# The row term of a graph-attention score, moved from TensorE transposes to a DMA through memory and a ScalarE copy

## What is computed

```python
mask = adjacency_matrix.astype(jnp.float32) + jnp.eye(n, dtype=jnp.float32) > 0
for l in range(attn_w.shape[0]):
    si = x @ attn_w[l, :d]
    sj = x @ attn_w[l, d:]
    scores = si[:, :, None] + sj[:, None, :] + attn_b[l]
    scores = jnp.where(scores >= 0, scores, 0.2 * scores)
    scores = jnp.where(mask, scores, -jnp.inf)
    attn = jax.nn.softmax(scores, axis=-1)
    agg = jnp.einsum('bij,bjd->bid', attn, x)
    h = layernorm(x + agg, g1[l], beta1[l])
    ff = jax.nn.gelu(h @ W1[l] + b1[l], approximate=False) @ W2[l] + b2[l]
    x = layernorm(h + ff, g2[l], beta2[l])
```

## Time and profile before

| | |
|---|---|
| median of 3 runs | 2259.94 us (2259.12 to 2261.8) |
| the profiled execution | 2259.16 us, span of its trace 2257.0 us |
| busy in the span | PE 97%, DVE 83%, ACT 84%, POOL 85% |
| chain that ended last | PE 83% of the span, DVE 12% |
| mean granted TensorE clock | 0.997 of full speed |
| DMA | 144.71 MB, 64 GB/s over the span |

### The profile page before, as it was taken

How to read it: one execution, slowest core, us unless ns; L and a number is a source line. 1 busy time by engine, 2 the same in 40 slices (tenths; PEclk the granted TensorE clock), 3 DMA queues, 4 the chain that set the end, 5 groups by cost and what they waited for, 6 DMA issues and landing times.

```text
span 2257.0 us, 46173 instructions
## 1 busy us (share of the span) xinstructions
PE 2199.1 (97%) x15464; PEld 1520.3 (67%) x15464; DVE 1868.8 (83%) x5886; ACT 1887.4 (84%) x3496; POOL 1914.8 (85%) x1644
## 2 busy tenths in 40 slices
PE   3999999999999999999999999999999999999998
PEld 2666766666666666666666666666666666666665
DVE  6889887788998787878999877777899978787874
ACT  5888888889888888888889888888898988888874
POOL 5788888889998888888999888888999888888896
PEclk9999999999999999999999999999999999999999
DMA  5432221135562112213654221122456221211253
GB/s 145 119 82 52 52 36 38 35 61 97 105 121 52 38 34 39 34 38 71 111 108 98 48 37 36 37 36 41 87 109 125 46 41 34 39 34 38 52 94 66
DMA packets 382266, 144.71 MB, mean 64 GB/s; under 512 B 312144, under 2 KB 380368, under 8 KB 382032
## 3 DMA queue, kind: packets, MB, share of 16 engines
q1 hardware_dynamic: 366192, 126.04, 27.3%
q0 software_dynamic: 15840, 15.73, 4.8%
HBM read 49.96 MB, written 16.78 MB: 30 GB/s over the span
## 4 chain that ended last, share of the span: by engine, by line
PE 83%; DVE 12%; issue 2%; DVEq 0%
PE p_hid L459 38%; PE p_pair L473 37%; PE p_pair L511 5%; DVE g_lo L712 2%; DVE bn L719 2%; PE p_pair L497 2%; DVE res L795 2%; DVE adj_in L740 2%; DVE dots L757 1%; DVE dots L760 1%; DVE p_lo L807 1%; PE p_pair L484 0%; DVE mv L724 0%; DVE var_eps L726 0%; DVE s_j L760 0%
## 5 line engine op out<-in xcount | busy, mean ns | idle before, releaser
L473 PE MATMUL p_pair<-w_hi,g_hi 128*128 128x256 f16 x3072 | 837.4, 273 | 0.0
L473 PE MATMUL p_pair<-w_hi,g_lo 128*128 128x256 f16 x3072 | 837.4, 273 | 0.0
L473 PE MATMUL p_pair<-w_lo,g_hi 128*128 128x256 f16 x3072 | 837.4, 273 | 0.0
L577 ACT ACTIVATE p_hid<-p_hid,b_eff 128x512 f32<-128x512 f32 x768 | 503.4, 655 | 282.7 <-PE p_hid L459 281.1
L712 DVE TENSOR_TENSOR g_lo<-p_hid,g_hi 128x512 f16<-128x512 f32 x768 | 517.4, 683 | 43.5 <-ACT g_hi L582 35.6
L459 PE MATMUL p_hid<-hT_hi,w_hi 128*128 128x512 f16 x1536 | 458.6, 380 | 22.1 <-DVE g_lo L712 17.4
L582 ACT ACTIVATE g_hi<-p_hid 128x512 f16<-128x512 f32 x768 | 458.7, 597 | 24.3
L459 PE MATMUL p_hid<-hT_lo,w_hi 128*128 128x512 f16 x1536 | 457.8, 380 | 0.5 <-DMA hT_lo<-h_lo 0.3
L459 PE MATMUL p_hid<-hT_hi,w_lo 128*128 128x512 f16 x1536 | 458.1, 380 | 0.0
L981 POOL TENSOR_TENSOR rstd<-var_eps,minus_half 128x4 f32<-128x4 f32 x224 | 228.5, 1020 | 244.3 <-DVE minus_mean L727 244.1
L473 PEld LDWEIGHTS p_pair<-w_hi,g_hi 128*128 128x128 f16 x3072 | 300.6, 98 | 106.5 <-issue 0.3
(11 more groups left out here) (77 smaller groups left out, 3574.0 us busy)
## 6 DMA issues: line engine op xcount, KB each, us to landing
out<-w_f SPq DMA_DIRECT2D x31, 512.0 KB, 4.1
x_in<-in_x SPq DMA_DIRECT2D x30, 512.0 KB, 6.9
w_f<-in_x POOLq DMA_DIRECT2D x30, 512.0 KB, 7.6
adj_in<-in_adj SPq DMA_DIRECT2D x32, 256.0 KB, 3.3
w_f<-in_L_gnn_W SPq DMA_DIRECT2D x6, 1024.0 KB, 7.0
hT_hi<-h_hi SPq DMA_TRANSPOSE x96, 3.1
hT_lo<-h_lo SPq DMA_TRANSPOSE x96, 3.1
pT_hi<-p_hi SPq DMA_TRANSPOSE x94, 2.4
```

The costliest lines, as they stand in the source:

```text
L473: mm = pe.matmul(ff_banks(s)[:, t, :], g[i][:, nodes], w[l][:, c, :], start=(c == 0 and t % 2 == 0 and n == 0), stop=(c == C - 1 and n == ...
L577: act.activation(p_hid[k][:], p_hid[k][:], ACT.Gelu, bias=b1_eff[:, l, c:c + 1], scale=1.0 / WSCALE).then_inc(gelu_ready, 1)
```

## The change

The row term of items 4 and on is no longer made by PE. SP writes `s_j` (128 partitions by 4 numbers) to a small buffer in memory, graph by graph, then reads those 512 numbers back as one row of 2 KB onto every partition (`sj_rows`), and ACT copies that tile into the PSUM bank where the transposes wrote before. `add_scores` reads the bank as before.

ACT's copy comes at c = 2 of slot s for item s+3, ahead of `norm_attention`. PE's wait for `res2` of item s-1 goes from PE's stream, and the same wait stands ahead of the copy in ACT's stream. To give the way through memory its time, the dot products run a slot earlier (item s+5 in slot s), and with them `norm_input` (s+5), `input_statistics` (s+6) and the loads of x. `make_mask` stays at s+4. The bias fold writes to another bank half, all of it in one slot, and PE's wait for it moves to `aggregate`.

In the opening `first_input(3)`, half of the low weights and the sum of two residual rows leave their places: the sum is now an adding DMA from POOL, `low_weights(0, 3)` and `first_input` of items 4, 5 and 6 lie in slot 0, whose DVE stream also has the dot products of items 4 and 5.

```diff
+        sj_rows = sb("sj_rows", [P, T, N])
+        sj_memory = [nc.dram_tensor(f"sj_memory{i}", [T, N], F32).ap() for i in range(2)]
...
+            def sj_to_memory(r, s):
+                sp.wait_ge(dots_ready, total(r, s, 8, 8))
+                if later(r, s, 6):
+                    sp.wait_ge(sj_in, sj_total(r, s - 2))
+                with nc.allow_non_contiguous_dma("four bytes of each node and graph"):
+                    sp.dma_start(sj_memory[s % 2].rearrange("t n -> n t"), s_j[s % RING][:]).then_inc(sj_out, 16)
+
+            def sj_to_rows(r, s):
+                sp.wait_ge(sj_out, sj_total(r, s))
+                if later(r, s, 5):
+                    sp.wait_ge(sj_rows_ready, total(r, s - 1, 1, 1))
+                sp.dma_start(sj_rows[:].rearrange("p t n -> p (t n)"),
+                             sj_memory[s % 2].rearrange("t n -> (t n)").partition_broadcast(P)).then_inc(sj_in, 16)
+
             def slot(r, s):
+                first = isinstance(r, int) and (r, s) == (0, 0)
+                if is_item(r, s + 4) and not first:
+                    sj_to_memory(r, s + 4)
                 if is_item(r, s + 2):
                     turn_probs_hi(r, s + 2)
...
-                if is_item(r, s + 4) and layer_of(s + 4) == 0 and group_of(r, s + 4) + 2 < G:
-                    sp.wait_ge(x0_ready, group_total(r, s + 4, 4, 4))
-                    load_x(group_of(r, s + 4) + 2)
+                if is_item(r, s + 5) and layer_of(s + 5) == 0 and group_of(r, s + 5) + 2 < G:
+                    sp.wait_ge(x0_ready, group_total(r, s + 5, 4, 4))
+                    load_x(group_of(r, s + 5) + 2)
                 if is_item(r, s + 1):
                     turn_h_lo(r, s + 1)
...
+                if is_item(r, s + 4):
+                    sj_to_rows(r, s + 4)
...
             def spread_sj(r, s):
 
                 pe.wait_ge(dots_ready, total(r, s, 8, 8))
-                if later(r, s, 4):
-                    pe.wait_ge(res2_ready, total(r, s - 4, 2, 2))
...
-                    if c == 4 and is_item(r, s + 3):
-                        spread_sj(r, s + 3)
+                    if isinstance(r, int) and (r, s, c) == (0, 0, 4):
+                        spread_sj(0, 3)
...
+            def rows_to_bank(r, s):
+                act.wait_ge(sj_in, sj_total(r, s))
+                act.wait_ge(res2_ready, total(r, s - 4, 2, 2))
+                act.activation(sj_bank(r, s), sj_rows[:], ACT.Copy).then_inc(sj_rows_ready, 1)
+
...
+                    if c == 2 and is_item(r, s + 3) and later(r, s):
+                        rows_to_bank(r, s + 3)
                     if c == 2 and is_item(r, s + 1):
                         norm_attention(r, s + 1)
...
-                    if c == 3 and is_item(r, s + 4) and layer_of(s + 4) == 0:
-                        norm_input(r, s + 4)
+                    if isinstance(r, int) and (r, s, c) == (0, 0, 3):
+                        norm_input(0, 4)
+                    if c == (4 if isinstance(r, int) and (r, s) == (0, 0) else 3) and is_item(r, s + 5) and layer_of(s + 5) == 0:
+                        norm_input(r, s + 5)
...
-                starts = is_item(r, s + 5) and layer_of(s + 5) == 0
+                starts = is_item(r, s + 6) and layer_of(s + 6) == 0 and not (isinstance(r, int) and (r, s) == (0, 0))
...
-                    if c == 6 and is_item(r, s + 4):
-
-                        dot_products(r, s + 4, 0)
-                        dot_products(r, s + 4, 1)
+                    if isinstance(r, int) and (r, s, c) == (0, 0, 4):
+                        low_weights(0, 3)
+                        dot_products(0, 4, 0)
+                        dot_products(0, 4, 1)
+                    if c == 6 and is_item(r, s + 5):
+
+                        dot_products(r, s + 5, 0)
+                        dot_products(r, s + 5, 1)
...
                 first_input(2)
-                first_input(3)
                 first_residual(0)
                 dot_products(0, 1, 0)
                 dot_products(0, 1, 1)
                 low_weights(0, 0)
+                low_weights(0, 1)
                 first_scores(1)
-                low_weights(0, 1)
+                first_input(3)
```

More of the change, by code:

```diff
@@ L379, in slot @@
                     weights(2, (s - 5) // 2)
+                if first:
+                    sj_to_memory(r, s + 4)
+                if is_item(r, s + 4):
+                    sj_to_rows(r, s + 4)
             def attention_rows(layers):
@@ L506, in aggregate @@
                     pe.wait_ge(score_steps, total(r, s + 1, 5, 4))
+                if isinstance(r, int) and r == 0 and s + 1 in FOLD_AT:
+                    pe.wait_ge(bias_ready, FOLD_AT[s + 1] + 1)
                 if later(r, s, 3):
@@ L860, in slot @@
                         hidden(r, s, c)
-                    if isinstance(r, int) and (r, s, c) == (0, 0, 0):
-                        first_input(4)
                     if c == 0 and is_item(r, s + 2):
@@ L874, in slot @@
                         dot_products(0, 3, 1)
+                    if isinstance(r, int) and (r, s, c) == (0, 0, 2):
+                        first_input(4)
+                    if isinstance(r, int) and (r, s, c) == (0, 0, 3):
+                        first_input(5)
                     if isinstance(r, int) and (r, s, c) == (LOOPS, PER - 1, 3):
@@ L895, in slot @@
                         aggregates(1, total(r, s + 2, 10, 8))
[L896 to L899 removed]
+                    if isinstance(r, int) and (r, s, c) == (0, 0, 4):
[5 more added lines that the diff above has]
+                        dot_products(r, s + 5, 1)
+                    if isinstance(r, int) and (r, s, c) == (0, 0, 7):
+                        first_input(6)
                     if isinstance(r, int) and (r, s, c) == (0, 2, 7):
@@ L1061, in slot @@
                     low_X(r, s + 2)
+                if first:
+                    first_deviation(5, 0)
                 if is_item(r, s + 1):
@@ L1066, in slot, with residual_rows @@
                     first_mask(s + 4)
+            def residual_rows(layers):
+                pool.dma_start(res_rows[:, layers].rearrange("p l d -> p (l d)"),
+                               b2[layers].rearrange("l d -> (l d)").partition_broadcast(P),
+                               accum_op=ALU.add).then_inc(res_rows_ready, 16)
             def first_deviation(i, n):
```

80 lines of the change are left out of this document (39 added, 41 removed).

## The result

The changed kernel takes **2293.8 us** (2292.6 to 2295.8) against 2260.0 for the kernel before on the same chip: ratio 1.0151, with a 95% interval of 1.0139 to 1.0163. It is 34 us slower. The forecast was 2279 in a range of 2236 to 2298. The profiled executions have spans of 2290.7 and 2257.0.

A forecast was written before the change was run, and what follows sets the result against it. PE's stream, busy 97% of the span, was taken as the bound, with DVE the bound in turn slots. Transposes -26, opening -6 and turns +52 gave +20 on 2259.16, so 2279 us, range 2236 to 2298.

The forecast's parts named there:

- 55 plain slots: Slots 8 to 18, 29 to 42, 53 to 66, 77 to 92: each loses PE's 0.44 us of transposes, 24.2 in all.
- slots 28, 52, 76: Slots with the mask but, after the change, neither statistics nor norm: from 22.80 to 22.15 us, 2.0 gained in all.
- three turns: Slots 19 to 27, 43 to 51, 67 to 75, layer 2 to 0: ACT's wait delays DVE, +17.3 us each, +52 together.
- opening to the end of slot 7: First slots: two waits bound the gain at 11 us, DVE's added work costs 7.1; taken as -6, ends -12 and +3.
- three waits in a full slot: Turn slots with mask, statistics and norm: DVE waits 1.9, 1.2 and 0.55 us for high halves of chunks 3, 4, 5.
- the mask's 0.21: In slots 28, 52 and 76: the delay by the mask, counted as gone after the change along with the transposes.
- R: Mid-slot time when DVE ends res2 of item s-1, for which ACT's copy waits; 1121.13 in slot 46.
- 6 us of room: The rows' two DMAs per item: 22 - 10 - 6 leaves 6 us before ACT wants them, so they cost nothing.
- The wait doesn't bind: Rival for the turn slots: ACT's lateness meets no one, so turns lose the transposes too; 2213 us, chance 10%.
- DVE's instructions get shorter: Rival for the turns: POOL's idle time shortens mask and low_probs, full slots 24.4 to 24.8; 2239 us, chance 14%.
- PE goes slower: Rival for some 20 turn slots: pauses drop PE to the 1.2 GHz level, up to 1.3 us each; 2305, chance 8%.
- The rows come late: Rival for every slot: the first DMA takes much longer than 5.4 us and ACT stands; 2330 or more, chance 3%.

The follow-up runs named there:

- e3: The kernel before with only ACT's wait for the residual of item s-1 added ahead of the attention norm, no copy or DMA: 2310.4 us, ratio 1.0225.
- e1: The changed kernel with ACT's copy and its wait moved from chunk 2 to behind chunk 3: 2228.2 us, ratio 0.9862 to the kernel before.
- e2: The changed kernel with the attention norm put ahead of ACT's wait and copy at chunk 2: 2243.4 us, ratio 0.9928 to the kernel before.
- e5: The changed kernel with the transposes back on PE, without DMAs, copy and its wait; reordered opening and slot-ahead order kept: 2254.3 us, ratio 0.9973.
- e6: The kernel with the copy behind chunk 3, with item 4's row term on PE and without its write and rows: 2221.6 us, ratio 0.9831.
- e4: The kernel with the copy behind chunk 3, with item 4's rows issued behind the probabilities' transposes in slot 1: 2230.2 us, ratio 0.9865.
- e8: The kernel with the copy behind chunk 3, with the DMA that brings the rows back issued twice per item: 2228.4 us, ratio 0.9866.

## Why the prediction was right in its sign, and 15 us short

Term by term, from the slots' own lengths in the two profiled executions:

| term of the sum | predicted | measured |
|---|---|---|
| 55 plain slots | -24.2 | -21.3 |
| slots 28, 52, 76 | -2.0 | +1.0 |
| three turns | +52 | +52.0 |
| opening to the end of slot 7 | -6 | +2.0 |
| sum | +20 | +33.7 |

**The turns: right, in mechanism and size.** The three waits in a full slot were put at 1.9, 1.2 and 0.55; they are 2.06, 1.02 and 0.49. A full slot was put at 26.35 and takes 26.39, one with the mask and the norm at 24.5 and takes 24.40, the nine at 225.7 and take 225.7. e3 shows that the wait alone does it, e1 that without its place nothing else does, e2 that the first wait goes by itself and leaves the other two. That the 225.7 is met to the tenth is luck: from residual to residual the same nine take 227.8 and not 227.05 (slot 19 takes 23.9 instead of 23.5, slot 27 23.2 instead of 22.8), and what is more there falls into slot 28. The step that carried this was to go through ACT's queue behind the wait and compare each high half with the time at which DVE wants it.

**Plain slots: right for 52 of 55.** They take 22.15. Slots 9 to 11 take 22.79, 23.18 and 23.16. The step that failed is the count: the slots behind the opening were called plain without looking at what else stands in them (weights are split up to slot 11, and DVE is busy 19.93 in slot 10 instead of 17.55); in e1 the same three take 22.15, so it is the wait that they pay for.

**Slots 28, 52 and 76: wrong by 1.0 each.** The prediction let them lose the transposes and the mask's 0.21 as well. They kept the mask's part (22.38 in e1) and had 0.8 of the wait on top (23.16). The mask alone makes DVE late enough for R to matter; the prediction had said so for slot 27 and not for the next.

**The opening: mis-sized by 8.** Up to the start of slot 8, the reordering brings -2.5 (e5; the prediction had -4), the seven transposes -3.1 (7 x 0.44). Against these stand two costs. Slot 1 of the changed kernel takes 29.11 and not e5's 25.54 less 0.44, which is +4.0:

```profile
71.37:100.48 29.11, 23.00 (x157) 14.80 (x158) 24.47 (x86) 22.50 (x47) 17.55 (x13) 1.00 0.64 147
```

PE stands there 2.64 us for the low probabilities' transpose and 1.02 for a `g_lo`. Slots 2 to 7 take 145.15, and 141.45 in e1, where ACT's wait stands a chunk later: +3.7. In e3 the wait alone costs these six slots 4.0. Together that is +2.1, and +1.96 was measured. So two steps failed. The DMA was costed at nothing in a plain slot, by 6 us of room, and the opening was never gone through with it: there the first write needs some 12 us and not 5.4, with five loads of rows for the other layers issued just ahead of it, and what is queued behind SP's wait is wanted at once. And the wait for R was to take some of 3 us in slots 1 to 3; it took 3.7, 3.3 of it in slots 5 to 7, where weights are split as in slots 9 to 11.

The prediction's own range for the sum, 2264 to 2297, isn't what the ends of its terms add up to, 2260 to 2296.

**The rivals.** *The wait doesn't bind*: no, but 2213 for a kernel without it was near: e6 takes 2221.6. *DVE's instructions get shorter*: the mask in slot 46 still takes 1.38 us, in a slot 3 us longer, as in the earlier trace rows. POOL stood idle elsewhere in the slot, but beside the mask (1130.02 to 1131.40) it was at its output rows (from 1128.17 to 1134.20 without a pause). By the rule of the Trainium skill named in the prediction ("SBUF — State Buffer", "Who interferes with whom") POOL's place in time counts, not its share of the slot, and the unchanged 1.38 agrees. The prediction's other number was misread: beside the 0.43 of the opening (from 7.58) POOL wasn't idle but at a deviation (L981, 128x4, 7.03 to 8.42), and in slot 22 of e1 the mask takes 0.59 (from 558.50) while POOL ends its `norm` (L1045, until 558.82). So the 0.43 doesn't bear the rule out as the prediction had it, and these cases don't go by whether POOL works; which of its instructions lengthen the mask, no run separates. *PE goes slower*: not in these turns, where PE stops for some 1 us at a time (once for 1.45, in slot 69) and the granted clock stays 1.00; it did in slot 1 of e1, and below is another place. *The rows come late*: not in the changed kernel, where in all 92 copies the releaser was DVE's residual; they did in the opening of e4.

## What to carry to other kernels

A wait has a price for all that is queued behind it on its engine, so go through that queue and ask of each result when its reader wants it; here one wait moved by one chunk was worth 66 us, while the copy and the transfer that it guards were free behind the opening, even twice over. An engine at 84% of a span has no room in the stretches where its partner is the bound. When a transfer is moved onto a shared queue, go through the first slots apart: there the same DMA meets the loads of the opening, and whoever stands on its landing holds up the transfers behind it.

## What the runs showed of the hardware that was not expected

**A short stop in a turn of e1 costs more than itself.** Slot 73 waits 2.36 us for the transpose of h's low half and takes 26.36, 1.05 more than the 22.95 of the slot before it (72) and the wait together. PE's timeline there:

```profile
1699.47 0.27 PE L501 MATMUL p_pair<-w_hi,g_lo 128*128 128x256 f16 x1
...
1702.97 0.93 PE L487 MATMUL p_hid<-hT_lo,w_hi 128*128 128x512 f16 x2 [2.36 <-DMA hT_lo<-h_lo]
1703.69 0.42 PE L501 MATMUL p_pair<-w_hi,g_hi 128*128 128x256 f16 x1
```

The feed's matmul takes 0.42 and not the 0.27 it takes just ahead of the stop; the granted clock was 1.00 before, 0.50 from 1704 to 1706, the 1.2 GHz level, and 1.00 again from 1708. In the changed kernel PE loses more in a full slot, in pieces of 1.0 and less, and its clock stays at 1.00: here the pieces were cheaper than one stop. Not every longer stop does this: behind the 2.64 us in slot 1 of the changed kernel the granted clock is 1.00.

The stops on h's transpose add up to 2.9, 3.9 and 4.5 us in the three turns of e1, which take 204.2, 206.0 and 208.6; DVE's busy time goes the same way, 187.8, 190.8 and 192.9 (the mask of slot 22, above, is one of the shorter instructions). Which of the two sets the lengths, no run separates. Twice the rows' traffic doesn't lengthen these stops (e8 has 11.4 us of them in all, e1 11.8), but e5, which has no rows and slower slots, has 1.2. What makes that transpose land after 7 to 9 us in a turn, and after 7 in e5 too, stays open.
